# Attention's turns behind the first expert tile: an order of work inside a slot, on TensorE and ScalarE

## What is computed

```
x = layernorm(x + attention(x, x, x, causal))            # self attention, 16 heads of 8
x = layernorm(x + attention(x, ctx, ctx, not causal))    # cross attention
x = layernorm(x + moe(x))                                # 8 experts, best 2 of each token
moe: router = softmax(x @ rw + rb); the two largest, their weights by softmax again
     h = gelu(x @ w1[e] + b1[e]); y = h @ w2[e] + b2[e]; out = sum of y times weight
```

## Time and profile before

| | us |
|---|---|
| median of 3 runs | 783.73 |
| lowest, highest | 779.12, 784.22 |
| the profiled execution, its own time | 778.71 |
| its span in the profile | 776.9 |

### The profile page before, as it was taken

One profiled execution on the slowest core, in us unless ns is written; L12 is line 12 of the kernel. 1 busy time (PEld: TensorE's weight loads), 2 busy tenths in 40 slices (PEclk: granted clock), 3 DMA queues, 4 the chain that ended last, 5 costly groups with the idle time before them and its releaser, 6 DMA issues. The chain is left out here.

```text
span 776.9 us, 21266 instructions
## 1 busy us (share of the span) xinstructions
PE 582.8 (75%) x7870; PEld 463.6 (60%) x7870; DVE 489.1 (63%) x1337; ACT 452.1 (58%) x824; POOL 370.7 (48%) x576
## 2 busy tenths in 40 slices
PE   2666777587677889878988988688777776888970
PEld 1344555455445577756776766577566666777970
DVE  4465999759978677787875778865334741121163
ACT  1224645435434599977997889688467654344310
POOL 7132243414367434427753664587247566540350
PEclk9986989869987899998999999799999889899995
DMA  4462575733234455544755666446555457788720
GB/s 105 118 180 63 160 216 162 259 95 110 69 89 138 143 177 152 173 134 134 227 148 167 188 175 188 129 151 191 155 156 184 157 176 223 246 275 262 237 84 20
DMA packets 141413, 124.64 MB, mean 160 GB/s; under 512 B 12224, under 2 KB 123600, under 8 KB 141312
## 3 DMA queue, kind: packets, MB, share of 16 engines
q1 hardware_dynamic: 134496, 113.06, 48.4%
q0 software_dynamic: 4368, 9.05, 4.1%
q10 hardware_dynamic: 2448, 1.18, 0.5%
HBM read 86.81 MB, written 38.54 MB: 161 GB/s over the span
## 5 line engine op out<-in xcount | busy, mean ns | idle before, releaser
L1100 DVE TENSOR_REDUCE row_max<-bank 128x16 bf16<-128x1024 f32 x64 | 78.2, 1222 | 55.2 <-PE bank L1512 54.3
L1648 PE MATMUL bank<-w_in,w_hl 128*128 128x128 f32 x704 | 102.9, 292 | 0.0
L781 POOL TENSOR_TENSOR prob_lo<-probT,prob_hi 128x384 f16<-128x384 f32 x64 | 69.2, 1081 | 70.3 <-ACT prob_hi L897 69.9
L1648 PEld LDWEIGHTS bank<-w_in,w_hl 128*128 128x128 f32 x704 | 90.4, 201 | 0.3
L894 ACT ACTIVATE probT<-bank 128x1024 f32<-128x1024 f32 x64 | 65.6, 1024 | 41.5 <-PE bank L1536 40.7
L767 POOL TENSOR_TENSOR veps<-mv,eps 128x1 f32<-128x1 f32 x64 | 14.2, 222 | 139.8 <-DVE mv L1138 139.8
L804 POOL DMA_INDIRECT w_hl<-ys,pos x60 | 59.8, 996 | 39.3 <-DMA ys<-w_hl 22.2
L1634 PE MATMUL bank<-xT,w_in 128*128 128x128 f16 x1056 | 76.7, 225 | 0.0
L1093 DVE TENSOR_TENSOR prob_lo<-probT,prob_hi 128x640 f16<-128x640 f32 x64 | 60.4, 944 | 24.9 <-ACT prob_hi L897 24.9
L946 ACT ACTIVATE w_hl<-bank 128x512 f32<-128x512 f32 x88 | 52.6, 597 | 36.8 <-PE bank L1634 36.2
L790 POOL DMA_INDIRECT xs<-x_hl,pos x60 | 62.9, 1049 | 17.8 <-issue 17.8
(11 more groups left out here) (173 smaller groups left out, 1521.1 us busy)
## 6 DMA issues: line engine op xcount, KB each, us to landing
w_in<-w_scr SPq DMA_DIRECT2D x96, 512.0 KB, 3.6
q_scr<-q_hl SPq DMA_DIRECT2D x64, 128.0 KB, 2.2
k_scr<-k_hl SPq DMA_DIRECT2D x64, 128.0 KB
q_st<-q_scr SPq DMA_DIRECT2D x32, 256.0 KB, 3.9
k_all<-k_scr SPq DMA_DIRECT2D x128, 64.0 KB, 2.1
xs_tile<-xs SPq DMA_DIRECT2D x42, 128.0 KB, 3.8
ys<-w_hl SPq DMA_DIRECT2D x42, 128.0 KB, 2.1
xs<-xs_tile SPq DMA_DIRECT2D x3, 1472.0 KB, 6.8
```

Source lines behind the costliest of these rows:

```text
L781: pool.tensor_tensor(p_lo[u.buf][:, h, :], probT[u.buf][:, h, :], p_hi[u.buf][:, h, :], ALU.subtract).then_inc(lo_second[u.kind], 1)
L1100: dve.reduce_max(row_max[u.buf][:, :], bank[:, SC:SC + 2, :].rearrange("p a (h k) -> p (a h) k", k=S), AX.X).then_inc(max_done[a], 1)
L1648: last = pe.matmul(expert_y(x), hid[x.par][:, c, :], w2_t[x.wb][:, c, :], start=False, stop=c == FC - 1, skip_group_check=True)
```

## The change

turns_late(slot) no longer asks whether the slot has tiles. It is now true in slots -5 to 50, 52 to 66 and 68 to 76. On PE, turn_both in a late slot stands behind turn_tile and up of the slot's first tile; it stood right behind the scores. On ACT, copy_turned of the next tile comes first, then both_turned, then gelu and copy_y; tile_step is written out for this.

```diff
 def turns_late(slot):
-    return not tiles_in(slot) and chunk_closes(slot) is None and slot < ATTENTION_END
+    return chunk_closes(slot) is None and slot < ATTENTION_END
...
                 if u := unit_at(g - 1):
                     exps(u, same_buffers(g - 1))
+                for x in tiles[:1]:
+                    if y := x.near(1):
+                        copy_turned(y)
                 if turns_late(g):
                     both_turned(g)
                 for x in tiles[:1]:
-                    tile_step(x)
+                    gelu(x)
+                    if y := x.near(-1):
+                        copy_y(y)
...
                     scores_T(g, u)
                 if u := unit_at(g):
                     scores(g, u)
-                if turns_late(g):
-                    turn_both(g)
                 for x in tiles[:1]:
                     if y := x.near(1):
                         turn_tile(y)
                     up(x)
+                if turns_late(g):
+                    turn_both(g)
                 u, v, c = unit_at(g - 2), unit_at(g - 5), routed_at(g, 2)
```

## The result

The changed kernel takes 817.92 us in the median of four runs (815.74 to 820.82), beside 781.42 us for the kernel before: a ratio of 1.0462, 95% interval 1.0427 to 1.0497. The forecast was 801, a price of 17 us, with a range from 783 to 818; the price measured is 36.5, and 817.92 lies at the very end of that range. Direction and mechanism were right, and a little over half of the price was missing. The profiled execution took 817.61 us with a span of 815.8, at a mean granted clock of 0.878 (0.901 before).

The account below looks back on a forecast made before the run. ScalarE's chain was taken to bound one-tile slots, VectorE the routing slots. The terms 20.9+1.1-1.5-0.5-5.0+0+2 = +17 us gave 795.7 for the profiled execution, 801 on the scale of the runs, with a range from 783 to 818.

Parts of the forecast that it names:

- Scores win nothing in one-tile slots; ScalarE is the bound: One-tile slots: scores no longer wait for the turns, but exp still starts when ScalarE has loaded its table; no gain.
- The hole of 0.86 us before oT: Late slots: turns wait for ScalarE's xT copy, so ScalarE idles 0.86 us before oT, which starts at E+3.07.
- The later second layer and the new lengths: One-tile slots: down starts at E+3.85, or E+4.96 with logits; periods 8.07, 8.37, 9.82, 8.95 for g%4 = 1, 2, 3, 0.
- The round of four: Four successive one-tile slots, one of each g%4, together growing from 30.50 to 35.2 us.
- The sum of the one-tile slots, +20.9: One-tile slots with attention outside the routing: added lengths 9.3+0.4+3.4+7.8 = +20.9 us.
- Two-tile slots, +1.1: Slots 53, 55, 57, 62: exp 1.49 us sooner at the end, against a second layer 1.49 or 2.60 later; together +1.1.
- Slots 50 and 51, -0.5: Slot 51 stays early: about +1.0 us in slot 50 and -1.5 behind 51, together -0.5.
- Slot 33, -1.5: Start of slot 33: wins the same 1.5 us as two-tile slot ends, since slot 32 was late already.
- Routing, -5.0: Slots 42 to 44 and 58 to 60: scores no longer held behind TensorE's wait for o_n; -2.5 us each, -5.0 together.
- Slots 64 to 76, 0, ends -6 and +6: Last slots: those without exps may win 0.7 us each, those with exps lose; taken as 0, ends -6 and +6.
- The clock term, +2 (ends 0 and +18): TensorE's new 1.5 to 2 us hole before xT in each slot: clock cost +2 us, ends 0 and +18.
- the clock rival: Same waits, but the clock also falls to about 0.85 in these slots, +18 us over about 30 slots: 817 to 819; chance 0.11.

Follow-up runs that it names:

- fill: The changed kernel plus six 128x512 matmuls ahead of the first layer in late slots with logits: 801.01 us, ratio 1.0252 to the kernel before.
- logits_behind_fill: The changed kernel with logits behind weigh and out_proj on TensorE, plus six 128x512 matmuls ahead of the first layer in late logits slots: 780.20 us, ratio 0.9988.
- logits_behind: The changed kernel with TensorE doing weigh and out_proj ahead of the logits: 792.66 us, ratio 1.0130 to the kernel before.

## Why the forecast was right, and why its size was not

- *Scores win nothing in one-tile slots; ScalarE is the bound:* right. Exp starts behind the table load in them, as before. The slots with g%4 = 1 stayed as they were where they had been 8.00 long (+0.07); 41 and 45, which I had counted with them though they took 7.57 and 7.28, rose to 8.23 and 8.07.
- *The hole of 0.86 us before oT:* right, 0.86 or 0.87 us in each late slot from 34 to 63. TensorE's wait for xT is there too, 1.39 and 2.12 us; its wait for o_n is not wholly gone, as I had said it would be, 4.7 us are left in front of L1565.
- *The later second layer and the new lengths:* right where the clock stayed up. Forecast 8.07, 8.37, 9.82 and 8.95; measured 8.07 in slots 37 and 49, 8.37 in 34 and 46, 9.84 in 63, 8.78 in 52 and 56; 8.55 in slot 38 was 0.18 over. That half of the slots carries the forecast. The round of four, forecast at 35.2 us, came to 39.7 (slots 36 to 39), and ScalarE's wait before the projections' copies, forecast at 0.5 us, to 1.43 in slot 39: both are the slots at the lower level.
- *The sum of the one-tile slots, +20.9:* they grew by 32.1. Of this 10.2 us are what slots 35, 36, 39, 40, 47 and 48 took over their forecast lengths, at clocks of 0.85 to 0.69; 21.9 is left.
- *Two-tile slots, +1.1:* +3.4, of which 2.4 are slot 55's over its forecast (clock 0.76); 1.0 is left. The end of slot 53, against the earlier trace rows, in ScalarE's timeline of the changed kernel:
```profile
466.19 0.28 ACT L954 ACTIVATE w_hl<-bank 128x128 f32<-128x128 f32 x1 [0.63 <-PE bank L1653]
466.49 1.28 ACT L894 ACT_TABLE_LOAD   x1
468.00 1.02 ACT L894 ACTIVATE probT<-bank 128x1024 f32<-128x1024 f32 x1 [0.23 <-PE bank L1541]
```
  The 0.86 and the two copies are gone, as said; exp now comes 1.81 behind L954's start, not 1.59, for scores_T became the later input by 0.23.
- *Slots 50 and 51, -0.5:* -1.7. *Slot 33, -1.5:* not to be told, as the stretch ahead of it varies by more.
- *Routing, -5.0:* -1.7. The second gave -2.2 for the -2.5 forecast. The first gave +0.5. Exp of slot 44 did come 1.62 us behind the x_hl copy (371.36 to 372.98), 3.6 sooner than in the earlier trace rows, but on the way there slot 43 ran its second layer at the lower level and took 12.21, and slot 44 took 10.42. In fill these two took 11.42 and 8.78, so I put 2.4 of the miss of 3.0 down to the clock; this is an estimate, for fill's slot 42 lost the clock instead (12.25 us against 9.98), and its slots 42 to 44 together take 32.4 us as in the change (32.6). In the second routing the clock of slot 59 was 0.69 before and 0.85 with the change, so its agreement is not the waits alone.
- *Slots 64 to 76, 0, ends -6 and +6:* +2.5 to slot 72's exp, where the clock went from 0.94 to 0.89, and +4.5 behind it, up to the end of the kernel. Of the latter I can only say that the same stretch ranges from 176.3 to 182.6 us over all kernels, and from 178.1 to 181.4 over those that turn as before in slots 72 to 76. It stays open.
- *The clock term, +2 (ends 0 and +18): this is the step that failed.* It comes to 10.2+2.4+2.4 = 15 us, the six one-tile slots, slot 55 and the estimate for slots 43 and 44; fill and logits_behind_fill bear out the one-tile part. I weighed two rows, one at 1.00 with 3.2 us of holes in two slots and one at 0.85 with holes of 2 to 3 us, and went by the busy share, 77%, which was that of the first. The share told nothing: slot 38, 83% busy, ran at 1.00 and slot 39, 76% busy, at 0.72, while the row of 186 to 200 had 77% at 1.00. More telling in the changed kernel is the form of the holes. All 14 late logits slots from 34 to 63 have the second one of 0.81 us, with five matmuls between; the clock fell in the ten whose first hole was 1.42 us or more (35, 36, 39, 40, 43, 44, 47, 48, 55, 59) and stayed at 1.00 in the four where it was 0.61 to 1.26 (52, 56, 60, 63). It is no rule: in fill slots 39, 43, 47, 55 and 59 lost it with a first hole of 0.80 to 1.06, and in logits_behind seven of the ten lost it without the second. Why one slot loses the clock and another does not stays open; what is shown is that the loss comes with these holes and makes up the excess. My own numbers held both holes, the wait for xT and then the wait for x2_tile, and I added them as waits without asking what they do to the clock together.

The forecast gave the clock rival 0.11 and 817 to 819 us; the kernel took 817.92. It is my main mechanism with this rival's price, and the check that the forecast named for it, a clock under 0.9 in the round, came out at 0.83 for slots 36 to 39 (292.47 to 332.20). That the number fits so well is luck: the rival spread at most 1.2 us over some 30 slots with a hole each, where the clock in fact cost 1.2 to 2.4 us in seven logits slots and about 1.2 in two more, and the 7 us behind slot 63, which the forecast had put at 0, stay unexplained. It is luck too that 817.92 fell inside the range, by 0.08 us. The rule that the forecast cited against itself, in the Trainium skill's "TensorE: Matmul & The Clock Gate", section "HAM oscillation — how this bites in real kernels", holds that bursts parted by idle gaps lose the fast clock again and again. This case's trace agrees, in ten of 14 late logits slots and at a cost of about 15 us, though that section's gaps are waits for DMA and those here are waits for ScalarE's copies, of 0.8 to 2.4 us.

## What to carry to other kernels

When an order of work is changed, list the idle gaps that it makes on TensorE, one after another, and give a slot that gets gaps as here (1.4 to 2.4 us, with or without 0.8 us behind) a second price, with the matmuls behind them at the lower level (here 1.2 to 2.4 us per slot), and do not go by the mean busy share. Where several uses share one bank, count the hand-overs in a row: a copy, a transpose and the next copy is a full exchange (0.86 us here, 0.45 for a transpose of two matmuls), and it should lie under work that does not need it. Late turns shortened only the slots at the routing, where the input came late anyway, and some ends of two-tile or closing slots; a change of order is worth trying slot by slot.

## What the chip showed that I had not expected

- Adding matmuls made the program faster: six extra ones in the logits slots took the sum of eight slots from 91.2 to 80.7 us, and the clock of slot 36 from 0.69 to 1.00; over slots 34 to 63 about half of that was left, 5.4 us.
- The clock reacts to a small difference and not in a regular way. In fill, slots 35 and 39 run the same work in the same order; one was at 1.00 and 9.84 us, the other at 0.85 and 11.24. Slot 42 has the same two holes (1.54 and 1.06 us) in the change and in fill, and ran at 1.00 there and at 0.72 here. Which slot loses it could not be foreseen from the profile. This stays open.
- Stretches far ahead of any edit moved by several us from kernel to kernel (slot 34's exp at 267.4 to 275.1). Only a count by slots keeps this out of an experiment's result.
